# Two layers of Mamba and mixture-of-experts on one core: in the first layer a predicated copy picks each token's expert output, in place of a masking product

## What is computed

```python
router_probs = softmax(xt @ Wr + br)
gates = max(router_probs)
idx = argmax(router_probs)
onehot = one_hot(idx, E)
xn = layernorm(xt) * ln_g + ln_b
h = relu(einsum('te,td,edf->tf', onehot, xn, W1) + b1[idx])
y = einsum('te,tf,efd->td', onehot, h, W2) + b2[idx]
y = y * gates
```

## Time and profile before

| | us |
|---|---|
| median of 3 runs | 913.11 |
| lowest and highest | 912.3, 918.16 |
| profiled execution | 914.93 |
| its span in the profile | 913.1 |
| TensorE busy | 805.6 (88%) |
| VectorE busy | 682.9 (75%) |
| ScalarE busy | 420.7 (46%) |
| GpSimd busy | 490.3 (54%) |

### The profile page before, as it was taken

One profiled execution on the slowest core, in us unless ns is written; L12 is line 12 of the kernel. 1 busy time (PEld: TensorE's weight loads), 2 busy tenths in 40 slices (PEclk: granted clock), 3 DMA queues, 4 the chain that ended last, 5 costly groups with the idle time before them and its releaser, 6 DMA issues.

```text
span 913.1 us, 10705 instructions
## 1 busy us (share of the span) xinstructions
PE 805.6 (88%) x2312; PEld 383.6 (42%) x2312; DVE 682.9 (75%) x1096; ACT 420.7 (46%) x699; POOL 490.3 (54%) x388
## 2 busy tenths in 40 slices
PE   2858998999899988868998987999887999889997
PEld 1324444444444443333454343544343544344443
DVE  4389359927973845349879897789896889899995
ACT  2744554455455634555334633434542434563341
POOL 0086436634660553225756656656655656757773
PEclk9979999999999989998999999999998999999999
DMA  9265255332523553167744575756565745758771
GB/s 266 57 189 136 89 169 150 104 106 83 161 54 106 150 169 88 31 162 193 186 146 125 131 186 143 187 128 154 143 154 131 178 132 141 176 138 212 189 186 35
DMA packets 85851, 129.28 MB, mean 142 GB/s; under 512 B 7368, under 2 KB 28560, under 8 KB 85808
## 3 DMA queue, kind: packets, MB, share of 16 engines
q1 hardware_dynamic: 85808, 128.85, 53.7%
HBM read 125.35 MB, written 3.47 MB: 141 GB/s over the span
## 4 chain that ended last, share of the span: by engine, by line
PE 30%; DVE 16%; issue 11%; ACT 4%; DMA 3%; POOL 1%; DVEq 1%; SPq 1%; ACTq 0%; POOLq 0%
DVE state L619 6%; PE bank L1496 6%; PE bank L1504 5%; DVE bank L612 3%; PE bank L1359 3%; PE bank L1397 3%; DMA CB<-crow 3%; PE bank L1384 2%; PE bank L1386 2%; PE bank L1444 2%; PE bank L1385 2%; DVE gg L739 2%; PE bank L1314 1%; DVE hid L747 1%; ACT sg L1225 1%
## 5 line engine op out<-in xcount | busy, mean ns | idle before, releaser
L619 DVE TENSOR_TENSOR_SCAN state<-decay,bank 128x512 f32<-128x512 f32 x192 | 232.9, 1213 | 17.5 <-issue 9.1
L1384 PE MATMUL bank<-XH,wh 128*128 128x512 f32 x256 | 176.3, 689 | 25.5 <-DVE gg L739 11.1
L1496 PE MATMUL bank<-xw,wu 128*128 128x512 f32 x256 | 141.9, 637 | 36.5 <-DVE hid L747 36.2
L1179 ACT ACTIVATE decay<-delta,negA 128x510 f32<-128x510 f32 x192 | 135.7, 715 | 42.0 <-DVE state L619 41.7
L1186 ACT ACTIVATE hid<-bank,early 128x512 f32<-128x512 f32 x128 | 87.5, 685 | 142.0 <-PE bank L1444 132.2
L612 DVE TENSOR_TENSOR bank<-bank,CB 128x512 f32<-128x512 f32 x192 | 133.2, 694 | 20.6 <-DMA CB<-crow 11.5
L1444 PE MATMUL bank<-hid,wd 128*128 128x512 f32 x256 | 147.5, 659 | 0.0
L902 POOL TENSOR_TENSOR product<-state,CB 128x512 f32<-128x512 f32 x64 | 81.7, 1276 | 99.9 <-DVE state L619 99.9
L1504 PE MATMUL bank<-hid,wd 128*128 128x512 f32 x256 | 132.4, 600 | 0.0
L1225 ACT ACTIVATE sg<-bank 128x512 f32<-128x512 f32 x128 | 75.7, 592 | 99.9 <-PE bank L1386 99.9
L898 POOL TENSOR_TENSOR product<-state,CB 128x512 f32<-128x512 f32 x64 | 81.6, 1276 | 74.4 <-DVE state L619 44.4
(11 more groups left out here) (167 smaller groups left out, 922.6 us busy)
## 6 DMA issues: line engine op xcount, KB each, us to landing
CB<-crow SPq DMA_DIRECT2D x256, 256.0 KB, 5.0
CB<-crow SPq DMA_DIRECT2D x64, 512.0 KB, 4.8
cwb<-cwrow SPq DMA_DIRECT2D x32, 256.0 KB, 5.7
wu<-W_dram SPq DMA_DIRECT2D x8, 256.0 KB, 5.3
wd<-W_dram SPq DMA_DIRECT2D x8, 256.0 KB, 5.9
wu<-Wu_dram SPq DMA_DIRECT2D x8, 256.0 KB, 3.6
xw<-Wg_dram SPq DMA_DIRECT2D x8, 256.0 KB, 4.6
wd<-Wd_dram SPq DMA_DIRECT2D x8, 256.0 KB, 5.0
```

The costliest lines, as they stand in the source:

```text
L619: v.tensor_tensor_scan(state[:, c % RING, :], decay[:, c % RING, :], drive, 0.0, ALU.mult, ALU.add).then_inc(state_ready.sem, 1)
L1179: a.activation(by_batch(decay[:, c % RING, :])[:, :, 1:], by_batch(delta[:, m, :])[:, :, 1:], ACT.Exp, scale=negA[:, c:c + 1]).then_inc(de ...
L1384: t.matmul(dst, wh[:, e, ws], XH[:, :], start=True, stop=False)
L1496: t.matmul(bank[UP_BANK][:, :], wu[:, e, 128 * f:128 * f + 128], xw[:, e % 2, :], start=True, stop=True).then_inc(up_ps.sem, 1)
```

## The change

Hidden units lose the masking product: the third pass ends them. Each expert's output now has a bank of its own for four down products, UP_BANK for even and OUT_BANK for odd experts, and the first of them begins the bank afresh. VectorE copies an expert's output into `yfT` where the expert's one-hot row is not zero (`select`: a memset of one element per partition and a predicated copy). Selections 0 to 6 stand in slots 6, 10, ... 30, two slots after an expert's last unit, and selection 7 in slot 2 of the next pair. TensorE waits for selection e - 2 before it reuses a bank. The one-hot rows take the way that layer 1's weights take: to DRAM (`send_mask`, slot 18) and back spread over all partitions into the two rows of `cwb` (`load_mask`). At the start of layer 1 the fetches of cw wait for the last selections. The bias product and ScalarE's copy are gone; in slot 3 four products with the identity and four with b2, 128 columns each and alternating, write the transposed result with its bias into the head bank. The constants `big` and `ohm` go, and ynT passes through DX_BANK instead of UP_BANK, which TensorE does after the last drive. Line numbers behind the changed places shift by up to 37.

```diff
 LAG0, LAG1 = 2, 3
+SELECT_AT = FT + LAG0
...
+        def out_bank(e):
+            return (UP_BANK, OUT_BANK)[e % 2]
...
+            def load_mask(j, e):
+                if j > 0 or e >= CWR:
+                    sp.wait_ge(sel_ready.sem, sel_ready.at0(j, e - CWR + 1))
+                src = cwrow[j % 2, e:e + 1, :].to_broadcast((128, T))
+                sp.dma_start(cwb[:, e % CWR, :], src).then_inc(cw_in[e % CWR].sem, 16)
+            def send_mask(j):
+                sp.wait_ge(*use0(head_read, j, "onehot"))
+                sp.dma_start(cwrow[j % 2, :, :], ohT[:, :]).then_inc(cw_out.sem, 16)
+                sp.wait_ge(cw_out.sem, cw_out.at0(j, 16))
             def load_cw(j, e):
...
+                if j == 0 and e < CWR:
+                    sp.wait_ge(sel_ready.sem, sel_ready.at0(PAIRS - 1, E - CWR + e + 1))
                 if j > 0 or e >= CWR:
...
             for e in range(E):
                 load_wd(e, w["W2"][e])
...
                 load_x(0 if last else i + 1, int(last))
                 for c in range(ROWS):
                     load_cb0(i, c)
+                load_mask(i, 0)
                 for u in range(UNITS):
+                    if u == LAG0 + 1:
+                        load_mask(i, 1)
+                    if u >= SELECT_AT + 1 and (u - SELECT_AT - 1) % FT == 0 and (u - SELECT_AT - 1) // FT + CWR < E:
+                        load_mask(i, (u - SELECT_AT - 1) // FT + CWR)
...
                         load_residual(i, 0)
                     for step in now(HEAD1 if last else HEAD0, u):
+                        if step == "onehot":
+                            send_mask(i + 1)
...
                     load_x(i + 1, 1)
                 if i == 0:
                     load_cw(0, 0)
-                load_cw(i, 1)
+                else:
+                    load_cw(i, 1)
                 for c in range(ROWS):
                     load_cb1(i, c)
+                if i == 0:
+                    load_cw(0, 1)
...
-                dve.wait_ge(*use0(head_read, i, "onehot"))
-                v.tensor_scalar(ohm[:, :], ohT[:, :], 1.0, None, ALU.subtract).then_inc(ohm_ready.sem, 1)
+            def select(i, e):
+                dve.wait_ge(cw_in[e % CWR].sem, cw_in[e % CWR].at0(i, 16 * (e // CWR + 1)))
+                dve.wait_ge(down_done.sem, down_done.at0(i, FT * e + FT))
+                dve.wait_ge(sel_ready.sem, sel_ready.at0(i, e))
+                if e == 0:
+                    dve.wait_ge(yf_ps.sem, yf_ps.at0(i, 0))
+                v.memset(pause[:, e % 2:e % 2 + 1], 0.0)
+                v.copy_predicated(yfT[:, :], cwb[:, e % CWR, :].bitcast(mybir.dt.int32), bank[out_bank(e)][:, :]).then_inc(sel_ready.sem, 1)
...
                 if late:
                     late(u)
+                if units and u >= SELECT_AT and (u - SELECT_AT) % FT == 0:
+                    select(i, (u - SELECT_AT) // FT)
...
                 if u == LATE:
-                    dve.wait_ge(mix_ps.sem, mix_ps.at0(i, 0))
+                    dve.wait_ge(yf_ps.sem, yf_ps.at0(i, 0))
...
             def late0(i, u):
+                if u == LAG0:
+                    select(i, E - 1)
...
             def late0(i, u):
-                if u == 1:
-                    act.wait_ge(mix_ps.sem, mix_ps.at0(i, 1))
-                    a.activation(yfT[:, :], bank[OUT_BANK][:, :], ACT.Copy).then_inc(yfT_ready.sem, 1)
...
                 pe.wait_ge(hid_ready.sem, hid_ready.at0(i, bank_free(u)))
-                three_passes(dst, e, f, False)
-                if u == 0:
-                    pe.wait_ge(ohm_ready.sem, ohm_ready.at0(i, 1))
-                t.matmul(dst, big[:, e:e + 1].to_broadcast((E, 128)), ohm[:, :], start=False, stop=True).then_inc(hid_ps.sem, 1)
+                three_passes(dst, e, f, True).then_inc(hid_ps.sem, 1)
...
-                if u == 0:
-                    pe.wait_ge(yfT_ready.sem, yfT_ready.at0(i, 0))
-                if u % FT == 0:
-                    pe.wait_ge(wd_in[u // FT].sem, wd_in[u // FT].at0(0, 16))
+                e, f = u // FT, u % FT
+                if f == 0:
+                    pe.wait_ge(wd_in[e].sem, wd_in[e].at0(0, 16))
+                    pe.wait_ge(sel_ready.sem, sel_ready.at0(i, e - 1))
                 pe.wait_ge(hid_ready.sem, hid_ready.at0(i, u + 1))
-                t.matmul(bank[OUT_BANK][:, :], wd[:, u, :], hid[:, u % 2, :], start=(u == 0), stop=False).then_inc(down_done.sem, 1)
+                t.matmul(bank[out_bank(e)][:, :], wd[:, u, :], hid[:, u % 2, :], start=(f == 0), stop=(f == FT - 1)).then_inc(down_done.sem, 1)
...
                         pe.wait_ge(yn_ready.sem, yn_ready.at0(i, 1))
-                        transposes(bank[UP_BANK], lambda k: yn[:, k, :], ynT_ps)
+                        pe.wait_ge(drive_ready.sem, drive_ready.at0(i, N))
+                        transposes(bank[DX_BANK], lambda k: yn[:, k, :], ynT_ps)
...
             def late0(i, u):
                 if u < LAG0:
                     down0(i, UNITS - LAG0 + u)
-                if u == LAG0 - 1:
+                if u == 3:
+                    pe.wait_ge(sel_ready.sem, sel_ready.at0(i, E))
                     pe.wait_ge(ohF_ready.sem, ohF_ready.at0(i, 1))
-                    t.matmul(bank[OUT_BANK][:, :], b2[:, :], ohF[:, :], start=False, stop=True).then_inc(mix_ps.sem, 1)
-                if u == 3:
-                    transpose_mixture(in0(i), head_read.at0(PAIRS, 0) + len(BANK1) if i is PAIRS - 1 else head_read.at0(i + 2, 0))
+                    pe.wait_ge(head_read.sem, head_read.at0(PAIRS, 0) + len(BANK1) if i is PAIRS - 1 else head_read.at0(i + 2, 0))
+                    for k in range(TT):
+                        here = slice(128 * k, 128 * k + 128)
+                        t.matmul(hb[:, here], yfT[:, here], ident[:, :], start=True, stop=False)
+                        last = t.matmul(hb[:, here], ohF[:, here], b2[:, :], start=False, stop=True)
+                    last.then_inc(yf_ps.sem, 1)
             def up1(i, u):
                 e, f = u // FT, u % FT
                 if f == 0:
                     pe.wait_ge(xw_ready.sem, xw_ready.at1(i, e + 1))
                 if u == 0:
...
                 t.matmul(bank[UP_BANK][:, :], wu[:, e, 128 * f:128 * f + 128], xw[:, e % 2, :], start=True, stop=True).then_inc(up_ps.sem, 1)
```

29 lines of the change are left out of this document (13 added, 16 removed).

## The result

The changed kernel takes 910.02 us (median of 13 runs, 905.79 to 914.37) where the kernel before takes 915.0 us (13 runs, 910.55 to 919.71): a ratio of 0.994, 95% interval 0.9916 to 0.9964. That is 5 us faster, clear of no change by the interval; the forecast was 10.5, to 902.6 us, reckoned from a median of 913.11.

A forecast was written before the change was run, and what follows sets the result against it. VectorE bounds layer 0's pairs from unit 6 to the one-hot, TensorE from there to y. Pair one -3.9, pairs two and three -3.4, pair four -6.2, layer 1 +3.0: -10.5 us, to 902.6, range 895 to 911.

The forecast's parts named there:

- Units 1.54 us apart: Sign in the changed profile: between the one-hot and y, units follow each other after 1.54 us, 0.53 less than before.
- one-hot to y: Stretch paced by TensorE: nine units lose 4.8 us, 0.5 comes back at the head bank, -4.3 in pairs one to three.
- 68 us: Rival, the plain count: TensorE bounds all of layer 0, all 128 masking products come off, 845 us; chance 0.03.
- Selection at 0.69: Sign in the changed profile: each selection, VectorE's predicated copy from bank to SBUF, takes 0.69 us.
- Two selections between xn and one-hot: Selections 1 and 2, where VectorE is full, add 0.66 us each in pairs one to three.
- the late row of expert 1: Layer 1's start: expert 1's weights are fetched only after selection 7, delaying GpSimd's products; +3.0 us, bounds 0 and +6.
- The contention rival: Selections' copies wait out GpSimd products at an SBUF interface: 17 x 1.26 = +21.4 us, so 924; chance 0.13.
- the step from the mixture to the gate: Units 0 to 5: the mixture takes 3.0 us, and the gate multiply comes 1.2 us later in pairs two to four.
- selection 0 at 0.66: Unit 6, where VectorE is full: memset and predicated copy together add 0.66 us in pairs one to three.
- the start, -1.0: Pair one: two units stand before the products the first scan needs, 2 x 0.53 = -1.0 us; mask fetches cost nothing.
- The clock at the one-hot: Rival: TensorE's wait before the one-hot lowers its clock, units 19 and 20 run at half speed, +9.2, so 912; chance 0.15.
- the fourth pair: Layer 0's last pair: +1.9 to xn, then -2.6, -4.2 and -1.3 behind it, together -6.2 us.

The follow-up runs named there:

- e1: The kernel before with the masking product left out of all 128 units, masks not applied: 889.28 us, ratio 0.9719.
- e6: The changed kernel with four rows in the buffer of masks instead of two: 906.93 us, ratio 0.9925 to the kernel before.
- e2: The changed kernel with unit 1's down product put ahead of the mixture's products in slot 3 of TensorE: 902.0 us, ratio 0.9851 to the kernel before.
- e3: The changed kernel with the mixture's four output bias products left out, biases not added: 900.48 us, ratio 0.9832 to the kernel before.
- e7: The changed kernel with unit 1's down product and the four bias products ahead of TensorE's wait for selection 7: 899.18 us, ratio 0.9836 to the kernel before.
- e4: The changed kernel with selection 0 put behind the small copy of the one-hot rows: 908.69 us, ratio 0.9935 to the kernel before.
- e12: The changed kernel with reordered down and bias products, selection 0 behind the small copy, four mask rows, later mask fetches and idle products in two waits: 889.54 us.

## Why the prediction was right or wrong

**Right.** What bounds the kernel: VectorE up to the one-hot, TensorE from there to y. Units 1.54 us apart (1.55), one-hot to y -4.4 at full clock, and 68 us refuted by e1. Selection at 0.69 (0.74). Two selections between xn and one-hot cost 1.05 where 1.3 was forecast. Layer 1: the late row of expert 1, product 14.0 us after XL (13 in the prediction's list, though its own 418.1 would be 15.8), +3.55 (+3.0), and +3.1 by e6 over many traces. The contention rival fell for the selections' copies: all 32 took 723 to 756 ns.

**Wrong, first: the step from the mixture to the gate, "they end at 219.8 instead of 218.5", and all behind it "1.2 us later. Bounds: 0 and 1.8".** The mixture itself was well sized in the third pair (3.3 against 3.0, end at XL + 10.6 against + 10.4). What failed is that what stands behind it moves by the same. The down product behind it took 2.08 us instead of 1.02, since the clock had gone to the 1.2 GHz level, and rectifier and tanh wait for it: 1.5 us by the mixture and 1.06 by the down product make the 2.54 of the gate in the third pair. In pairs two and four the clock fell within the mixture already, which took 3.5 and 3.9 us. The gate moved by 2.5 to 3.2 us, 4.8 us too much over three pairs, of which some 4 are the lower clock (3 x 1.06 + 0.2 + 0.6). That is more than the 4.0 us between the two sums; the other misses cancel, which is luck. The prediction had the clock as a rival at the one-hot only. The runs bear this out: with the down product ahead (e2), or with the clock kept up (e3, e7), the gate comes at 12.4 us or earlier.

**Wrong, second: selection 0 at 0.66.** The selection itself cost about 0.6 (e4: 18.6 against 18.0), but it pushed the small copy behind the start of a GpSimd product, which added 0.86 in pairs two and three. The prediction put the contention on the added instruction and not on its neighbours. GpSimd and VectorE in time order in the third pair:

```profile
229.39 0.74 DVE L623 COPY_PREDICATED yfT<-cwb,bank 128x512 f32<-128x512 int32 x1
...
229.72 1.27 POOL L951 TENSOR_TENSOR product<-state,CB 128x512 f32<-128x512 f32 x1 [0.91 <-DVE state L651]
...
230.02 1.25 DVE L673 COPY szm<-ohT 8x512 f32<-8x512 f32 x1
```

The copy starts 0.3 us after the product and ends 0.3 us after its end. The Trainium skill, "SBUF — State Buffer", section "Who interferes with whom", says that a copy which can enter a 2-port mode waits for the whole GpSimd instruction where that began first, and that an instruction with at most one SBUF input outside those modes does not. By that rule the small copy is held; the selection, whose data come from a bank, would be free if its mask counts as the one input. The small copy's row agrees. The selection shown began ahead of the product, so its row says nothing; but 12 of the changed kernel's 32 selections began inside a GpSimd product and took 723 to 756 ns, so they were not held.

**Wrong, third: the start, -1.0.** The first drive did come 1.0 us earlier after XL (18.15, before 19.15), but the next one waits for its CB row until 22.73 (before 22.48). What is late next is the transfer. I had asked whether the new fetches cost, not whether the old ones would be ready. From XL to xn pair one took 44.1 to 47.2 us in all these traces, and 45.7 in e1, which has no masks; why it is 1.1 us longer than before is open.

**The clock at the one-hot**, a rival with chance 0.15 at +9.2, is real at half the size: each occurrence costs 1.6 us and not 3.1, about one unit's time and not two, and it comes in half of the stretches. The wait, expected "under 3 us", was 2.0 or 3.66, and only the longer one is followed by long stretches. With 3.3 us in two of three fourth pairs it is some 4 to 5 us in a typical execution (0.5 x 3 x 1.6 + 0.67 x 3.3 = 4.6). The profiled execution had most of its draws at the good level, which fits with its lying below the median.

**Too small**: the fourth pair, -10.6 instead of -8.1. At the lower level it would have been about -7.3, close to the forecast. Both sums therefore depend on the level that this one execution happened to draw.

## What to carry to other kernels

When work on one engine grows, follow the order of the queue behind it to the first instruction that another engine waits for, and move that one ahead of the wait: here three lines of order (down product, grouping, biases first) were worth twice the gain of the change. Here it also paid to group small products of equal rows (2.2 us against 3.3, and the clock behind them stayed up in 17 of 18 cases, e7 to e12). Where a stretch paced by TensorE begins after a wait, idle products in the wait are worth a try: here, with waits of 3.65 us, they took 5.6 us off. Two lengths of the same stretch, in one trace or from trace to trace, are the sign to look for.
